# Expert weights of the last stage issued from SyncE behind each tile's value copies instead of from GpSimd

## The chip, the cores and the metric

One Trainium2 chip, one core of it. The time is the device time of one launch of the whole kernel in microseconds (us), the median of the runs shown.

## What is computed

Two transformer-like layers over x (64 batches of 32 tokens, 256 wide, so 2048 tokens), each with a cross attention, an attention and a feed-forward part. The change lies in the last two steps of the second layer: a causal grouped attention with 16 heads of 16 over 4 key/value groups, and a top-1 mixture of 8 experts.

```python
# attention of layer 1, on layernorm(x); g groups of keys and values, repeated for 4 heads each
kg = einsum('bse,ged->bgsd', x, Wk) + bk ; vg = einsum('bse,ged->bgsd', x, Wv) + bv
out = softmax(mask(q @ k.T / sqrt(16))) @ v
x = x + out
# experts of layer 1, on layernorm(x)
route = sigmoid(x @ router_w); e = argmax(route)
h = silu(x @ gate_w[e]) * (x @ up_w[e])          # 8 experts, 256 x 512 each
x = x + (h @ down_w[e]) * route[e]               # 512 x 256
```

The gate, up and down weights of one expert are 512 KB each in float32, so 4 MB for all gates, 4 MB for all ups and 4 MB for all downs.

## The kernel before, in words

The tokens lie in SBUF (`x_sb`) as 16 tiles of 128 rows, four batches of 32 tokens in a tile. Every stage of the kernel is one block in which each engine has its own instruction stream, and semaphores tie the streams together. The stage here is `attention_and_experts` (tensor names begin with `attn_` in the profile; `moe_gate`, `moe_up` and `moe_down` are the expert weights, `all_` and `w_` are tensors shared by stages). It runs from about 895 us to the end of the span.

**The attention half** is a software pipeline over the 16 tiles. In step i the TensorE stream does, in this order: scores of tile i (L2147, L2153), queries of tile i+1 (L2127), the transposes of the exponentials of tile i-1 (L2160), keys and values of tile i+1 (L2135, L2137), the transpose of the normalised tile i+2 (L2120), and last `weigh` of tile i-1 (L2171), the product of exponentials and values. The text calls the start of `weigh` of tile t W(t). The order is written out by hand in `step` of each engine; there is no scheduler.

**Values** take a detour. VectorE writes a tile's values (128 rows of 68 numbers, `v_rows`, L2407), SyncE copies them to DRAM (`v_stage`, L2001, 34 KB), waits until they have landed, and then issues four copies back into SBUF (`v_blocks`, L2005, 34 KB each), one for each of the four heads of a group, in the layout that `weigh` reads. `weigh` of tile t waits for these four copies. There are two buffers of each, so SyncE may start the four copies of tile t only when `weigh` of tile t-2 is done.

```python
for t in range(TILES):                       # SyncE before
    u = t % 2
    sp.wait_ge(s["v_ready"], t + 1)
    ...
    sp.dma_start(v_stage[u], ...)            # L2001
    sp.wait_ge(s["v_staged"], 16 * t + 16)
    wait_count(sp, s["o_made"], t - 1)
    for r in range(PER): sp.dma_start(v_blocks[u][...], v_stage[u]...)   # L2005, four
```

**Expert weights.** The gates are issued by SyncE at the end of the stage before (L2709, at 872 to 877 us). Ups and downs come from a generator, `load_ups_and_downs`, that issues one 512 KB load at each `next` (first the 8 ups, then the 8 downs, L2714). In the kernel before, GpSimd calls it twice in each of the iterations 1 to 8 of its own loop, right after it has normalised tile t (L2032). TensorE waits for all of them (`got_f`) only before the first expert slot, at about 1020 us.

**GpSimd** further adds the outputs of tile t-4 to x (L2037), writes the routing tables at iteration 3 (L2057 to L2063; VectorE waits for them in its step 0, L2457), and at the end computes the layernorm factors and the normalised rows (L140 to L147, L2042, L2077, L2079), after which ScalarE makes the rows of the middle tiles (L2328) and TensorE turns them (L2179) and routes (L2185).

**The expert half** begins at 1020 us: 23 slots, each with gate, up and down products (L2259, L2273).

Of the kernel before, what the change touches and what calls it, by code (L numbers as in the profile page):

```python
# [16 lines left out]
TILES = TOKENS // P  # L17
# [199 lines left out]
def wait_count(engine, semaphore, count):  # L217

    if not isinstance(count, int) or count > 0:
        engine.wait_ge(semaphore, count)  # L220
# [1674 lines left out]
EXPERTS, INNER = 8, 512  # L1895
# [3 lines left out]


def attention_and_experts(nc, name, scope, moments, x_sb, consts, ident, ident16, causal16, loaded, w, router_w, spare, room,
                          gate_w, up_w, down_w, load_pool, got_gates, got_f, out):


    sb, pb, sem = scope(name)
# [74 lines left out]
    def spare_of(n):  # L1980
        tiles = range(n * per_spare, min((n + 1) * per_spare, TILES))
        return tiles, spare[n][:, 0:len(tiles) * ROW].rearrange("p (t n) -> p t n", n=ROW)
# [9 lines left out]
    with nc.Block() as block:  # L1992

        @block.sync
        def _(sp):
            sp.wait_ge(s["blank"], 4)
            for t in range(TILES):
                u = t % 2
                sp.wait_ge(s["v_ready"], t + 1)
                wait_count(sp, s[f"v_in{u}"], 64 * (t // 2))  # L2000
                sp.dma_start(v_stage[u], v_rows[u][:, :, :].rearrange("p g d -> p (g d)")).then_inc(s["v_staged"], 16)  # L2001
                sp.wait_ge(s["v_staged"], 16 * t + 16)
                wait_count(sp, s["o_made"], t - 1)
                for r in range(PER):
                    sp.dma_start(v_blocks[u][SEQ * r:SEQ * r + SEQ, :, r, :, :].rearrange("k b g d -> k b (g d)"),  # L2005
                                 v_stage[u].rearrange("(b k) n -> k b n", b=TB)).then_inc(s[f"v_in{u}"], 16)

            out_tiles = out.rearrange("(t p) n -> p t n", p=P)
            for first, last in ((0, 12), (12, TILES)):
                sp.wait_ge(s["x_ready"], last)  # L2010
                sp.dma_start(out_tiles[:, first:last, :], x_sb[:, first:last, :]).then_inc(s["out_stored"], 16)

            normed_tiles = normed.rearrange("(t p) n -> p t n", p=P)
            for n in range(3):
                tiles, buffer = spare_of(n)
                wait_rows(sp, tiles[-1])
                if n == 1:
                    wait_rows(sp, EARLY[-1])
                if n == 2:
                    wait_rows(sp, MIDDLE[-1])  # L2020
                sp.wait_ge(s["prob_ready"], n + 2)
                sp.dma_start(normed_tiles[:, tiles.start:tiles.stop, :], buffer).then_inc(s["normed_stored"], 16)

        @block.gpsimd
        def _(pool):
            g = nc.gpsimd

            def normalise(t):
                if t == TILES - 1:
                    pool.wait_ge(s["dve_roots"], Moments.LAST_LINKS)  # L2030
                wait_count(pool, s["turned"], t)
                g.tensor_scalar(xn[:, :], x_sb[:, t, :], moments.moments[:, t, 0:1], moments.factors[:, t:t + 1],  # L2032
                                ALU.subtract, ALU.mult).then_inc(s["xn_ready"], 1)

            def add_outputs(t):
                pool.wait_ge(s["o_ready"], t + 1)
                g.tensor_tensor(x_sb[:, t, :], x_sb[:, t, :], outs[:, :, :].rearrange("p h d -> p (h d)"), ALU.add)\  # L2037
                 .then_inc(s["x_ready"], 1)

            def early_row(t):  # L2040
                pool.wait_ge(s["early_roots"], Moments.POOL_LINKS)
                g.tensor_scalar(rows(t), x_sb[:, t, :], moments.moments[:, t, 0:1], moments.factors[:, t:t + 1],  # L2042
                                ALU.subtract, ALU.mult).then_inc(s["early_rows"], 1)

            normalise(0)
            for u in range(2):
                g.memset(v_blocks[u][:, :, :, :, :], 0.0).then_inc(s["blank"], 1)
                g.memset(v_rows[u][:, :, HD], 1.0).then_inc(s["blank"], 1)
            loads = load_pool(pool)
            for t in range(1, TILES + POOL_LEAD - 1):  # L2050
                if t < TILES:
                    normalise(t)
                if t <= EXPERTS:
                    next(loads)
                    next(loads)
                if t == 3:
                    g.iota(count_rows[:, :], [[1, P]], 0, 0).then_inc(s["counted"], 1)  # L2057
                    g.iota(count_tiles[:, :], [[1, TILES]], -TILES, 0).then_inc(s["counted"], 1)
                    g.iota(count_p[:, :], [[1, 1]], 0, 1).then_inc(s["counted"], 1)
                    g.memset(ones16[:, :], 1.0).then_inc(s["tables16"], 1)  # L2060
                    g.memset(own16[:, TILES, :], 0.0).then_inc(s["tables16"], 1)
                    for u in range(2):
                        g.memset(x_in[u][:, :], 0.0).then_inc(s["x_in_clear"], 1)  # L2063
                if t >= POOL_LEAD:
                    add_outputs(t - POOL_LEAD)
                if t - POOL_LEAD == 10:
                    pool.wait_ge(s["early_stats"], 1)
                    pool.wait_ge(s["xn_ready"], len(EARLY))
                    moments.pool_roots(pool, s["early_roots"], EPS_LN, 1.0, EARLY)
                if t - POOL_LEAD in (11, 12, 13):  # L2070
                    for e in range(3 * (t - POOL_LEAD - 11), min(3 * (t - POOL_LEAD - 10), len(EARLY))):
                        early_row(e)
            pool.wait_ge(s["middle_stats"], 1)
            pool.wait_ge(s["xn_ready"], TILES)
            moments.pool_roots(pool, s["middle_roots"], EPS_LN, 1.0, MIDDLE)
            m = slice(MIDDLE.start, MIDDLE.stop)
            g.tensor_tensor(negated_mean[:, m], moments.moments[:, m, 0], moments.factors[:, m], ALU.mult).then_inc(s["mean_ready"], 1)  # L2077
            pool.wait_ge(s["mean_ready"], 1)
            g.tensor_scalar(negated_mean[:, m], negated_mean[:, m], -1.0, None, ALU.mult).then_inc(s["mean_ready"], 1)  # L2079

            def gather(j):
                g.indirect_dma_start(x_in[j % 2][:, :], None, normed, bass.IndirectOffsetOnAxis(token[:, j:j + 1], 0),
                                     bounds_check=TOKENS - 1, oob_is_err=False).then_inc(s[f"x_got{j % 2}"], 16)

            pool.wait_ge(s["x_in_clear"], 2)
            pool.wait_ge(s["normed_stored"], 16 * 3)
            pool.wait_ge(s["token_ready"], 1)
            gather(0)
            gather(1)
            pool.wait_ge(s["out_stored"], 32)  # L2090
            for j in range(SLOTS + 2):
                if j + 2 < SLOTS:
                    pool.wait_ge(s["x_turned"], j + 1)
                    pool.wait_ge(s["prob_kept"], j + 1)
                    gather(j + 2)
                if j >= 2:
                    pool.wait_ge(s["y_ready"], j - 1)
                    g.indirect_dma_start(out, bass.IndirectOffsetOnAxis(token[:, j - 2:j - 1], 0), y_out[j % 2][:, :], None,
                                         bounds_check=TOKENS - 1, oob_is_err=False, compute_op=ALU.add)\
                     .then_inc(s[f"y_stored{j % 2}"], 16)  # L2100
            for u in range(2):
                pool.wait_ge(s[f"y_stored{u}"], 16 * ((SLOTS + 1 - u) // 2))
# [450 lines left out]
def program(nc, d, out):  # L2553
# [9 lines left out]
    with outer:  # L2563
# [44 lines left out]
        got_gates, got_f = sem("got_gates"), sem("got_f")  # L2608

        era1 = outer.enter_context(ExitStack())  # L2610
        sb1, _, _ = scope("w", era1)
# [11 lines left out]
        def chunks(ap):  # L2623
            return ap.rearrange("(c p) n -> p c n", p=P)
# [36 lines left out]
        sb2, _, _ = scope("raw", era2)  # L2661
# [42 lines left out]
        sb3, _, _ = scope("moe", era3)  # L2704
# [3 lines left out]
            for e in range(EXPERTS):  # L2708
                sp.dma_start(f_gate[:, e, :, :], chunks(d["f_gate"][e])).then_inc(got_gates, 16)  # L2709

        def load_ups_and_downs(pool):
            for dst, src in ((f_up, d["f_up"]), (f_down, d["f_down"])):
                for e in range(EXPERTS):
                    pool.dma_start(dst[:, e, :, :], chunks(src[e])).then_inc(got_f, 16)  # L2714
                    yield

        phase = ExitStack()
# [95 lines left out]
```

## Time and profile before

| | |
|---|---|
| time, median of 3 runs | 1171.3 us (1168.67, 1171.3, 1177.4) |
| span of the profiled execution, first to last instruction | 1170.2 us |
| TensorE busy | 1105.2 us (94%) |
| attention half of the last stage | about 895 to 1004 us |
| expert half | about 1020 us to the end |

The profile shows one execution. Its span leaves out what lies around it; the median is 1.1 us above the span. A row of an engine's timeline gives the start, the time from the first start to the last end of the instructions on it, engine, line, operation, operands, how many, and in brackets how long the engine stood idle before and who released it.

### The profile page before, as it was taken

To read this page: it belongs to the slowest core of one execution; us is meant where nothing else is said; L and a number is where in the kernel's file an instruction comes from. 1 tells how busy PE (TensorE), PEld (TensorE's weight loads), DVE (VectorE), ACT (ScalarE), POOL (GpSimd) and SP (SyncE) were. 2 spreads that over 40 slices of the span, in tenths; PEclk is the share of its full clock that TensorE was granted. 3 is DMA by queue.
4 is the path that set the end of the run, shared out by engine and by line. 5 is a ranking of instruction groups with operands and counts; after the bars stand their busy time and mean duration, and the time that the engine had idled before them with its cause. 6 is when DMAs were issued, how large, how long until landed. Compare 5 with 4: busy or idle time off the path is not lost. (4 is left out here: it accounts for less than half of the span.)

```text
span 1170.2 us, 32565 instructions
## 1 busy us (share of the span) xinstructions
PE 1105.2 (94%) x12592; PEld 853.7 (73%) x12593; DVE 700.9 (60%) x1802; ACT 469.2 (40%) x1359; POOL 309.1 (26%) x421
## 2 busy tenths in 40 slices
PE   7998999999999899999979999999998798899996
PEld 6776878887887679889766777777765687556664
DVE  6897635445464665555448788887785587322221
ACT  2453535344352311212155565565552466222221
POOL 1701000000000000000253654655623547034442
PEclk9899999999999999999989999999999899799998
DMA  8631000000000055000101121121224643212211
GB/s 254 182 87 33 1 1 0 0 0 0 0 0 1 1 119 156 0 0 1 38 10 51 36 56 45 37 54 28 56 73 159 200 108 100 83 28 34 36 27 11
DMA packets 60205, 61.57 MB, mean 53 GB/s; under 512 B 26862, under 2 KB 51087, under 8 KB 59628
## 3 DMA queue, kind: packets, MB, share of 16 engines
q1 hardware_dynamic: 51836, 41.35, 13.3%
q0 software_dynamic: 8304, 19.32, 6.3%
q8 instruction: 45, 0.74, 0.3%
q14 instruction: 20, 0.16, 0.1%
HBM read 52.33 MB, written 10.14 MB: 53 GB/s over the span
## 5 line engine op out<-in xcount | busy, mean ns | idle before, releaser
L1729 ACT ACTIVATE xattn_exps<-xattn_ps_s,xattn_top 128x256 f32<-128x256 f32 x256 | 118.0, 475 | 76.9 <-DVE xattn_top L1797 76.9
L765 PEld LDWEIGHTS attn_ps_q<-attn_xnT,w_b_q 128*128 128x128 f32 x1024 | 118.8, 193 | 12.6 <-issue 12.6
L765 PE MATMUL attn_ps_q<-attn_xnT,w_b_q 128*128 128x128 f32 x1024 | 123.4, 276 | 0.0
L1255 POOL TENSOR_TENSOR fold_last_cos<-raw_last,all_consts 64x64 f32<-64x64 f32 x1 | 0.3, 317 | 453.5 <-POOLq L1063 453.5
L819 PE MATMUL attn_ps_out<-w_b_o,attn_oT 128*128 128x256 f32 x480 | 106.5, 380 | 1.8 <-DVE all_x L1000 1.5
L819 PEld LDWEIGHTS attn_ps_out<-w_b_o,attn_oT 128*128 128x128 f32 x480 | 90.0, 190 | 15.1 <-DVE all_x L1000 2.3
L873 ACT COPY attn_qT<-attn_ps_q 128x512 f32<-128x512 f32 x64 | 38.0, 594 | 148.2 <-PE attn_ps_q L765 148.2
L1804 DVE STREAM_TRANSPOSE xattn_expsT<-xattn_exps 128x1024 f32<-128x1024 f32 x64 | 79.5, 1241 | 22.9 <-ACT xattn_exps L1729 22.9
L1794 DVE TENSOR_REDUCE xattn_raw_top<-xattn_ps_s 128x4 f32<-128x1024 f32 x64 | 77.8, 1216 | 15.7 <-PE xattn_ps_s L1621 15.5
L1621 PE MATMUL xattn_ps_s<-xattn_kT,xattn_qT 64*32 64x256 f32 x2048 | 69.6, 381 | 2.9 <-ACT xattn_exps L1729 2.9
L1631 PE MATMUL xattn_ps_o<-xattn_expsT,xattn_kv 32*64 32x256 f32 x2048 | 64.1, 380 | 4.9 <-DVE xattn_last_scores L1840 3.5
L951 DVE BATCH_NORM_STATS2 attn_out_stats<-attn_ps_out 128x6 f32<-128x256 f32 x15 | 6.5, 432 | 99.6 <-PE attn_ps_out L819 99.6
L1596 PEld LDWEIGHTS xattn_ps_o<-xattn_xnT,all_d_a 128*128 128x128 f32 x512 | 61.5, 197 | 6.2 <-issue 6.2
L1596 PE MATMUL xattn_ps_o<-xattn_xnT,all_d_a 128*128 128x128 f32 x512 | 65.5, 283 | 0.0
L1631 PEld LDWEIGHTS xattn_ps_o<-xattn_expsT,xattn_kv 32*64 32x64 f32 x2048 | 44.4, 131 | 24.2 <-issue 11.9
L1094 PE MATMUL ffn_ps_h<-ffn_xnT,all_c 128*128 128x128 f32 x512 | 61.1, 278 | 0.0
L1111 PE MATMUL ffn_ps_out<-all_c,ffn_masked 128*128 128x256 f32 x256 | 59.6, 379 | 0.0
L1659 PE MATMUL xattn_ps_o<-all_d_b,xattn_ctxT 128*128 128x256 f32 x240 | 55.1, 382 | 4.4 <-POOL xattn_ctxT L1547 3.0
L1094 PEld LDWEIGHTS ffn_ps_h<-ffn_xnT,all_c 128*128 128x128 f32 x512 | 58.5, 192 | 0.0
L2544 DVE COPY all_d_b<-attn_ps_pT 128x512 f32<-128x512 f32 x23 | 15.9, 692 | 67.0 <-PE attn_ps_pT L2266 48.6
L1547 POOL TENSOR_TENSOR xattn_ctxT<-xattn_weighed_sum,xattn_inverse 128x256 f32<-128x256 f32 x60 | 42.8, 745 | 46.9 <-DMA xattn_inverse<-xattn_inverse_rows 46.9
L1621 PEld LDWEIGHTS xattn_ps_s<-xattn_kT,xattn_qT 64*32 64x32 f32 x2048 | 33.7, 106 | 27.3 <-issue 12.7
(359 smaller groups left out, 2322.0 us busy)
## 6 DMA issues: line engine op xcount, KB each, us to landing
xattn_inverse<-xattn_inverse_rows SPq DMA_DIRECT2D x30, 256.0 KB, 3.9
all_c<-in_ctx SPq DMA_DIRECT2D x64, 64.0 KB, 1.8
moe_gate<-in_f_gate SPq DMA_DIRECT2D x8, 512.0 KB, 8.1
moe_up<-in_f_up POOLq DMA_DIRECT2D x8, 512.0 KB, 5.2
moe_down<-in_f_down POOLq DMA_DIRECT2D x8, 512.0 KB, 5.5
xattn_v_stage<-xattn_v_rows SPq DMA_DIRECT2D x16, 136.0 KB, 2.0
xattn_v_blocks<-xattn_v_stage SPq DMA_DIRECT2D x64, 34.0 KB, 1.9
attn_v_blocks<-attn_v_stage SPq DMA_DIRECT2D x64, 34.0 KB, 1.9
```

Source lines behind the costliest of these rows:

```text
L765: last = nc.tensor.matmul(ps_q[g % 2][:, h * P:(h + 1) * P], wq[:, c, head * DH:(head + 1) * DH], xnT[u][:, c, :], start=(c == 0), stop=(c ...
L819: last = nc.tensor.matmul(bank[:, 0:DIM], of_heads[:, h, :, :].rearrange("p b q -> p (b q)"), wo[:, h, :], start=(h == 0), stop=(h == HEAD ...
L1094: last = nc.tensor.matmul(ps_h[half][:, j * P:(j + 1) * P], w1[:, c, f * P:(f + 1) * P], xnT[:, c, :], start=(c == 0), stop=(c == KC - 1))
L1111: last = nc.tensor.matmul(ps_out[:, 0:DIM], masked[u][:, f, :], w2[:, f, :], start=(f == 0), stop=(f == chunks - 1))
L1547: last = nc.gpsimd.tensor_tensor(ctxT[:, :, b, :], weighed_sum[:, :, b, :], inverse[:, b, :].rearrange("p (m q) -> p m q", q=SEQ), ALU.mult)
L1596: last = nc.tensor.matmul(ps_q[part][:, n * P:(n + 1) * P], a_w[:, c, m * P:(m + 1) * P], xnT[:, c, :], start=(c == 0), stop=(c == KC - 1))
L1621: last = nc.tensor.matmul(ps_s[g % 2][SEQ * b:SEQ * b + SEQ, 512 * odd + nkeys * n:512 * odd + nkeys * (n + 1)], qT[u][rows, b, 2 * g + n, :],
L1631: nc.tensor.matmul(ps_o[b][64 * odd:64 * odd + 64, 0:DIM], kv[u][rows, j, :], expsT[u][rows, :, odd, :, j, :], start=(j == 0), stop=False, ...
L1659: last = nc.tensor.matmul(out_bank(t), ctxT[:, m, :, :].rearrange("p b s -> p (b s)"), b_w[:, m, :], start=(m == 0), stop=(m == pairs - 1))
L1729: nc.scalar.activation(exps[g % 2][:, nkeys * k:nkeys * (k + 1)], ps_s[g % 2][:, nkeys * k:nkeys * (k + 1)], ACT.Exp, bias=top[u][:, n:n + ...
L1794: nc.vector.tensor_reduce(of_group(raw_top), ps_s[g % 2][:, :].rearrange("p (o m n) -> p o m n", o=2, m=2), X_AXIS, ALU.max, negate=True). ...
L1804: nc.vector.transpose(expsT[u][:, g, :, :, :, :].rearrange("p o m j q -> p (o m j q)"), exps[g % 2][:, :])\
```

## The change

The 16 loads of ups and downs leave GpSimd's loop. SyncE makes the generator's calls now: after the four value copies of tile t it issues no load for tiles 0 and 1, one for tiles 2 to 13, two for tiles 14 and 15. The order ups first, then downs, stays.

```diff
 def attention_and_experts(..., load_pool -> load_experts, ...)
         @block.sync
         def _(sp):
+            loads = load_experts(sp)
+
+            def loads_behind(t):
+                return 0 if t < 2 else 1 if t < TILES - 2 else 2
+
             sp.wait_ge(s["blank"], 4)
             for t in range(TILES):
...
                 for r in range(PER):
                     sp.dma_start(v_blocks[u][SEQ * r:SEQ * r + SEQ, :, r, :, :].rearrange("k b g d -> k b (g d)"),
                                  v_stage[u].rearrange("(b k) n -> k b n", b=TB)).then_inc(s[f"v_in{u}"], 16)
+                for _ in range(loads_behind(t)):
+                    next(loads)
...
-            loads = load_pool(pool)
             for t in range(1, TILES + POOL_LEAD - 1):
                 if t < TILES:
                     normalise(t)
-                if t <= EXPERTS:
-                    next(loads)
-                    next(loads)
...
-        def load_ups_and_downs(pool):
+        def load_ups_and_downs(sp):
             for dst, src in ((f_up, d["f_up"]), (f_down, d["f_down"])):
                 for e in range(EXPERTS):
-                    pool.dma_start(dst[:, e, :, :], chunks(src[e])).then_inc(got_f, 16)
+                    sp.dma_start(dst[:, e, :, :], chunks(src[e])).then_inc(got_f, 16)
                     yield
```

On SyncE, the first tiles of the stage before: the store of a tile's values and its four copies back follow each other with nothing between.

```order
L2001 DMA attn_v_stage<-attn_v_rows 128x68
L2005 DMA attn_v_blocks<-attn_v_stage 32x4x68 x4
L2001 DMA attn_v_stage<-attn_v_rows 128x68
L2005 DMA attn_v_blocks<-attn_v_stage 32x4x68 x4
L2001 DMA attn_v_stage<-attn_v_rows 128x68
```

On SyncE after the change, the last four tiles of the stage and what follows them (tiles 12 to 15; lines are 5 further down, `moe_` is the load).

```order
L2010 DMA attn_v_blocks<-attn_v_stage 32x4x68 x4
L2717 DMA moe_down<-in_f_down 128x4x256
L2006 DMA attn_v_stage<-attn_v_rows 128x68
L2010 DMA attn_v_blocks<-attn_v_stage 32x4x68 x4
L2717 DMA moe_down<-in_f_down 128x4x256
L2006 DMA attn_v_stage<-attn_v_rows 128x68
L2010 DMA attn_v_blocks<-attn_v_stage 32x4x68 x4
L2717 DMA moe_down<-in_f_down 128x4x256 x2
L2006 DMA attn_v_stage<-attn_v_rows 128x68
L2010 DMA attn_v_blocks<-attn_v_stage 32x4x68 x4
L2717 DMA moe_down<-in_f_down 128x4x256 x2
L2018 DMA out<-all_x 128x12x256
```

A load now stands between the value copies of one tile and the value store of the next, from tile 2 on; two stand there ahead of tile 15 and ahead of the stores of the output.

On GpSimd before, iterations 1 to 4 of its loop: a pair of loads follows each normalised tile, and the tables of iteration 3 stand behind the third pair.

```order
L2032 TENSOR_SCALAR attn_xn<-all_x,all_moments,all_moments_work 128x256
L2714 DMA moe_up<-in_f_up 128x2x512 x2
L2032 TENSOR_SCALAR attn_xn<-all_x,all_moments,all_moments_work 128x256
L2714 DMA moe_up<-in_f_up 128x2x512 x2
L2057 IOTA attn_count_rows 128x128
L2058 IOTA attn_count_tiles 128x16
L2059 IOTA attn_count_p 128x1
```

On GpSimd after, the same place.

```order
L2039 TENSOR_SCALAR attn_xn<-all_x,all_moments,all_moments_work 128x256 x3
L2060 IOTA attn_count_rows 128x128
L2061 IOTA attn_count_tiles 128x16
L2062 IOTA attn_count_p 128x1
```

The tables now follow the third normalised tile directly; the 16 load instructions are gone from this engine.

## Rows read from the trace of the kernel before

**Rows 1.** Busy time by stretch: us, engines' busy us (instructions), clock share, DMA, GB/s
```profile
912.00:924.00 12.00, 8.95 (x152) 7.41 (x152) 9.33 (x23) 7.18 (x20) 6.61 (x9) 1.00 0.72 221
924.00:936.00 12.00, 8.90 (x162) 7.21 (x163) 5.17 (x13) 3.58 (x11) 4.62 (x7) 0.72 0.50 132
...
948.00:960.00 12.00, 11.93 (x254) 9.62 (x254) 9.42 (x27) 8.25 (x23) 5.43 (x6) 1.00 0.23 44
...
927.00:932.00 5.00, 4.92 (x77) 3.95 (x78) 2.48 (x6) 0.16 (x1) 0.72 (x1) 0.52 0.68 203
```

**Rows 2.** TensorE's timeline: weigh of tiles 0 to 3, 7, 8, 14, and one query wait
```profile
911.30 0.68 PE L2171 MATMUL attn_ps_o<-attn_v_blocks,attn_expsT 128*32 128x68 f32 x32 [0.52 <-DMA attn_v_blocks<-attn_v_stage]
...
914.25 0.71 PE L2127 MATMUL attn_ps_q<-attn_xnT,all_e_q 128*128 128x128 f32 x4 [1.35 <-ACT attn_xnT L2299]
...
918.27 0.68 PE L2171 MATMUL attn_ps_o<-attn_v_blocks,attn_expsT 128*32 128x68 f32 x32 [0.76 <-DMA attn_v_blocks<-attn_v_stage]
...
927.08 1.14 PE L2171 MATMUL attn_ps_o<-attn_v_blocks,attn_expsT 128*32 128x68 f32 x32 [4.02 <-DMA attn_v_blocks<-attn_v_stage]
...
933.92 0.68 PE L2171 MATMUL attn_ps_o<-attn_v_blocks,attn_expsT 128*32 128x68 f32 x32
...
953.35 0.68 PE L2171 MATMUL attn_ps_o<-attn_v_blocks,attn_expsT 128*32 128x68 f32 x32
...
958.16 0.68 PE L2171 MATMUL attn_ps_o<-attn_v_blocks,attn_expsT 128*32 128x68 f32 x32
...
985.75 0.68 PE L2171 MATMUL attn_ps_o<-attn_v_blocks,attn_expsT 128*32 128x68 f32 x32 [0.30 <-issue]
```

**Rows 3.** SyncE's timeline: value stores and copies of tiles 2, 6 and 9
```profile
913.44 0.34 SPq L2001 DMA_DIRECT2D attn_v_stage<-attn_v_rows  x1
919.69 3.28 SPq L2005 DMA_DIRECT2D attn_v_blocks<-attn_v_stage  x4
...
938.72 0.34 SPq L2001 DMA_DIRECT2D attn_v_stage<-attn_v_rows  x1
942.39 1.73 SPq L2005 DMA_DIRECT2D attn_v_blocks<-attn_v_stage  x4
...
953.33 0.34 SPq L2001 DMA_DIRECT2D attn_v_stage<-attn_v_rows  x1
954.85 1.73 SPq L2005 DMA_DIRECT2D attn_v_blocks<-attn_v_stage  x4
```

**Rows 4.** The page's DMA issues: KB each, median us from issue to landing
```profile
xattn_inverse<-xattn_inverse_rows SPq DMA_DIRECT2D x30, 256.0 KB, 3.9
...
attn_v_blocks<-attn_v_stage SPq DMA_DIRECT2D x64, 34.0 KB, 1.9
```

**Rows 5.** Two downs on GpSimd at 935 us, and the gates: us from issue to landing
```profile
L2714 POOL DMA_DIRECT2D moe_down<-in_f_down x2: 760/784/809, 935.2 to 936.0; - x2
DMA to landing us min/median/max: 4.6/5.3/5.9
...
L2709 SPq DMA_DIRECT2D moe_gate<-in_f_gate x8: 469/540/792, 872.3 to 876.9; - x8
...
DMA to landing us min/median/max: 5.4/8.1/10.8
```

**Rows 6.** Stretches as in Rows 1: a pair of 256 KB loads; seven gates
```profile
855.00:857.60 2.60, 2.60 (x50) 2.13 (x30) 2.56 (x8) 1.54 (x6) 1.35 (x2) 1.00 0.78 212
...
877.70:886.00 8.30, 7.58 (x100) 5.38 (x99) 4.40 (x9) 2.05 (x9) 0.73 (x2) 1.00 1.03 380
```

**Rows 7.** GpSimd's and VectorE's timelines at the tables; GpSimd's and TensorE's at the end
```profile
907.90 1.49 POOL L2714 DMA_DIRECT2D moe_up<-in_f_up  x2
...
909.88 0.74 DVE L2457 CAST attn_of_row<-attn_count_rows 128x128 f32<-128x128 int32 x1 [3.48 <-POOL attn_count_p L2059]
...
988.37 0.73 POOL L2037 TENSOR_TENSOR all_x<-all_x,attn_outs 128x256 f32<-128x256 f32 x1 [0.30 <-DVE attn_outs L2416]
...
994.44 0.69 PE L2179 MATMUL attn_ps_kv<-all_consts,all_c 128*128 128x128 f32 x2 [2.02 <-ACT all_c L2328]
```

More of the change, by code:

```diff
@@ L1901, in attention_and_experts @@
 def attention_and_experts(nc, name, scope, moments, x_sb, consts, ident, ident16, causal16, loaded, w, router_w, spare, room,
-                          gate_w, up_w, down_w, load_pool, got_gates, got_f, out):
+                          gate_w, up_w, down_w, load_experts, got_gates, got_f, out):
     sb, pb, sem = scope(name)
```

## The prediction

> **What bounds the kernel now.** TensorE is busy 94% of the span, so I looked only for places where it is not, or where it is slow, in the stretch that the change touches. The view by stretches comes first [rows 1]: from 948 to 960 us TensorE is busy 11.93 of 12 us, while between 912 and 936 it is busy 8.95 and 8.90 of 12, and of the second 12 us it had only 0.72 of its clock. The DMA share is 0.72 and 0.50 there against 0.23 later: the 16 loads of ups and downs run in the poor stretch and not in the good one. Next TensorE's timeline [rows 2]. The start of `weigh`, W(t), is the pulse of the pipeline. W(8) minus W(7) is 958.16 - 953.35 = 4.81 us; the next gap in the steady part is 4.9, so I take 4.85 as the step when nothing is late. The first steps are W(1)-W(0) = 6.97, W(2)-W(1) = 8.81 and W(3)-W(2) = 6.84 us. The brackets name the causes: 0.52, 0.76 and 4.02 us of waiting for the value copies, and 1.35 us for ScalarE's xnT. After the 4.02 us of idleness the granted clock is 0.52 from 927 to 932, that is, the lower of its two levels (1.2 instead of 2.4 GHz) for most of it, and `weigh` takes 1.14 instead of 0.68 us.
>
> SyncE's timeline says why the copies are late [rows 3]. With no load in flight the store of tile 9 is issued at 953.33 and its copies at 954.85: 1.5 us for the store to land. For tile 6 it is 3.7 us (938.72 to 942.39), for tile 2 it is 6.2 us (913.44 to 919.69), and the four copies then take 3.28 us to issue instead of 1.73. The loads were issued by GpSimd and not by SyncE; yet the store of tile 6 lands at 942.4, just behind the second of two downs (936.0 + 5.9 = 941.9) [rows 5]. So a value store in effect waits until the loads ahead of it are in.
>
> **Part 1, GpSimd loses its loads.** The tables of iteration 3 stood behind a pair of loads of 1.49 us [rows 7], and VectorE stood idle 3.48 us until the tables were there, before it could turn the scores of tile 1. The tables come 1.49 us earlier, and VectorE's shift, ScalarE's exponentials and xnT behind it with them: of TensorE's 1.35 us about 0.9 goes (TensorE itself arrives 0.52 earlier at that point, so about 0.45 of waiting remains). Other pairs on GpSimd (7 of them, 1.5 us each) lay beside waits of GpSimd for TensorE and cost nothing.
>
> **Part 2, no loads beside the values of tiles 0 to 2.** Stores 0, 1 and 2 are free of ups and downs. The waits of 0.52, 0.76 and 4.02 us go, and with the idle gap the slow clock: W(3)-W(2) falls from 6.84 to 4.81, another 2.03. What is late next there is nothing, since a store that lands in 1.5 us puts a tile's copies in SBUF a full step before `weigh` wants them. Sum of the gain: 0.52 + 0.9 + 0.76 + 4.02 + 2.03 = 8.2 us. W(14), at 985.75 before, would be at 977.55.
>
> **Part 3, what the loads cost where they go.** They now stand in SyncE's own chain: four copies of tile t (1.73 us of issue, plus 0.04), the load, the store of tile t+1, and SyncE waits until that store has landed before it issues the copies of t+1. Call L the time from the issue of the load to the landing of the store behind it. One turn of SyncE takes 1.77 + L. TensorE's step is 4.85, so SyncE keeps up if L is at most 3.1; above that it falls behind by L - 3.1 a tile and uses up the slack first.
>
> The start: values of tile 2 are ready at about 912.0 (1.45 earlier than 913.4), the store lands 1.5 later at 913.5, and the load of tile 2 is issued at 915.3. The copies of tile 3 begin at 915.3 + L, those of tile 14 eleven turns later, and their last copy lands 3.3 later (it is issued 1.3 after the first and takes 1.9 [rows 4]). So W(14) is the later of 977.55 and 915.3 + L + 11 (1.77 + L) + 3.3 = 938.1 + 12 L. Fully hidden up to L = 3.29; even with before at L = 3.97; each 0.1 us of L is 1.2 us of time in between. I count to tile 14, since its output sets GpSimd's last addition at 988.37, the factors behind it and TensorE's restart at 994.44 [rows 7]; tile 15, which stands behind two loads, has the 2.02 us for which TensorE waits there as cover, and its extra (one more load, 1.4 us, and the longer turn, 0.8) just fits into that.
>
> L does not occur in the trace, since nothing was queued behind a single 512 KB load on SyncE. From below: a store alone takes 1.5, and the gates, eight in a row on SyncE's queue, land 1.43 us apart (872.3 + 5.4 = 877.7 to 876.9 + 10.8 = 887.7, over seven) [rows 5], so L is at least 1.5 + 1.4 = 2.9. From above: the first of a pair on GpSimd landed after 4.6 us, and store 6 landed 0.5 behind its load, so 5.1. The nearest row is a pair of 256 KB loads on SyncE (3.9 us to land [rows 4], the second issued 0.6 after the first, so 4.5 us for 512 KB). Their bytes moved in 2.6 us at 212 GB/s, the gates at 380 [rows 6], at which 524 thousand bytes take 1.4 us: 1.2 less, so a load lands after 3.3 and the store behind it 0.5 later, as store 6 did. This row is nearer than the ends, having the same queue and the same bytes, and I take L = 3.8: W(14) = 983.7, 2.1 us earlier than before. The issue itself, 0.5 to 0.6 us [rows 5], lies within L.
>
> For the landing of one load the Trainium skill ("DMA: Bandwidth & Descriptors", Anatomy of one DMA) fits 2.0 us plus the bytes over 436 GB/s, measured for GpSimd's path; as an estimate that is 3.2 us for 512 KB. The quicker of the two downs on GpSimd took longer, 4.6 [rows 5]. By the page L would be 3.7 and the gain 3.3 us in place of 2.1.
>
> **Part 4, the rest.** The output stores stand behind two loads (about 3 us); they are needed only by the expert half's additions after 1020 us. The last load is issued at about 990 and lands before 1000; TensorE wants it at 1020. Both cost nothing.
>
> **The rivals.**
> A, the forecast: SyncE's chain eats most of the gain, L from 3.4 to 4.2, that is 6.9 us earlier to 2.7 later, 1164.4 to 1174; 50%.
> B, the load is hidden: L up to 3.4. The lower bound 2.9 speaks for it, and that only one load is in flight at a time. Gain 6.9 to 8.2, 1163.1 to 1164.4. A bonus is possible: if TensorE's clock falls in the 2.02 us wait before 994.44 [rows 7], as it did after the 4.02 us, and tile 15 now fills that wait, the clock may hold. The slow level cost 2.0 us in a step of 6.84, so 3 us in the ten up to 1004, and the products behind it a little more. 22%, of which 4 with that and a time below 1159.6.
> C, slower: the SyncE chain becomes the bound of every step. The mechanism is the closed loop copies, load, store, landing; the price 12 us for each us of L; it decides from L = 3.97 on. For it speaks that stores took 3.7 to 6.2 us whenever loads were near. L from 4.2 to 5.1 gives 2.7 to 13.6 later, 1174 to 1185; 18%, 3 of them past 1%.
> D, the same loop with TensorE idle about 1 us in every step lets the clock fall, as the 4.02 us did; at the lower level a step costs 2.0 us more (6.84 against 4.81), over ten steps 20: about 1190. Against it: 1.35 us idle at 912.9 did not lower it (clock share 1.00 to 924). 7%.
> E, the loads were not what held the stores. The Trainium skill (same page, Queues, rings and completion order) says that each DMA engine takes turns between queues packet by packet, so that loads in GpSimd's queue should hardly delay a store in SyncE's, while in SyncE's own the store is behind the whole load; that speaks against this change. The row shows otherwise: 3.7 us against 1.5 with loads in the other queue, landing just behind them. If it held nevertheless, worked out from rows, the stall at 923 stays, L is the lower bound and hidden, and only the 0.9 of part 1 is won: 1170.4. 3%.
>
> **How the numbers follow.** The likeliest case is A at L = 3.8: 2.1 us off. The sum is made on the profiled span of 1170.2; carried over to the median of 1171.3 it gives 1169.2 us. The range takes B without its bonus and C up to L = 4.6: 1161 to 1179; outside it lie the bonus, D and the top of C, some 16%. One per cent, 11.7 us, is about what a measurement of this kernel can tell from no change. Faster by more: 4%. Slower by more (D and the top of C): 10%. Within: 86%.
>
> **What would show it.** In the changed profile no wait for `attn_v_blocks` at tiles 0 to 2 and a clock share of 1.00 from 900 to 936; the wait of VectorE for the tables 1.5 shorter. From tile 3 on the distance from a load's issue to the next copies on SyncE is L; if it is above 3.3, TensorE's waits for the value copies start after some tiles and repeat in each step, with W(t) going at 1.77 + L. If the copies are in time everywhere, B holds. The prediction is wrong if L is over 4.6, if the clock drops in the new short waits, or if the loads, moved later, touch something that I have called free.

## Result, and the profile after

| | before | after |
|---|---|---|
| time, median of 17 runs each | 1173.41 us | 1181.28 us |
| ratio to before, 95% interval | 1 | 1.0071, 1.0055 to 1.0086 |
| span of the profiled execution | 1170.2 us | 1177.1 us |

The change costs 0.7%, some 8 us. I had forecast a gain of 2 us (1169.2 us, range 1161 to 1179), with a loss of 3 to 14 us as rival C at 18% and one of about 20 us as rival D at 7%. The measured 1181.28 us lies above the range and within rival C.

TensorE's timeline after the change, the starts of `weigh` (compare [rows 2]):

```profile
912.73 0.68 PE L2174 MATMUL attn_ps_o<-attn_v_blocks,attn_expsT 128*32 128x68 f32 x32
...
914.85 0.71 PE L2130 MATMUL attn_ps_q<-attn_xnT,all_e_q 128*128 128x128 f32 x4 [0.51 <-ACT attn_xnT L2302]
...
918.12 0.68 PE L2174 MATMUL attn_ps_o<-attn_v_blocks,attn_expsT 128*32 128x68 f32 x32
922.93 0.68 PE L2174 MATMUL attn_ps_o<-attn_v_blocks,attn_expsT 128*32 128x68 f32 x32
...
938.00 0.68 PE L2174 MATMUL attn_ps_o<-attn_v_blocks,attn_expsT 128*32 128x68 f32 x32 [0.36 <-DMA attn_v_blocks<-attn_v_stage]
943.98 0.68 PE L2174 MATMUL attn_ps_o<-attn_v_blocks,attn_expsT 128*32 128x68 f32 x32 [1.19 <-DMA attn_v_blocks<-attn_v_stage]
949.69 0.68 PE L2174 MATMUL attn_ps_o<-attn_v_blocks,attn_expsT 128*32 128x68 f32 x32 [0.81 <-DMA attn_v_blocks<-attn_v_stage]
...
987.46 0.68 PE L2174 MATMUL attn_ps_o<-attn_v_blocks,attn_expsT 128*32 128x68 f32 x32 [3.67 <-DMA attn_v_blocks<-attn_v_stage]
...
992.22 1.14 PE L2174 MATMUL attn_ps_o<-attn_v_blocks,attn_expsT 128*32 128x68 f32 x32 [0.31 <-DMA attn_v_blocks<-attn_v_stage]
...
1001.46 1.13 PE L2174 MATMUL attn_ps_o<-attn_v_blocks,attn_expsT 128*32 128x68 f32 x32 [2.45 <-DMA attn_v_blocks<-attn_v_stage]
...
1005.35 0.69 PE L2182 MATMUL attn_ps_kv<-all_consts,all_c 128*128 128x128 f32 x2 [0.31 <-ACT all_c L2331]
```

The early stall is gone: tiles 0 to 2 wait for nothing (4.02 us before), and the wait for xnT (the turned normalised tile that ScalarE writes) is 0.51 instead of 1.35. VectorE's wait for the tables fell from 3.48 to 1.95 us, the 1.5 that part 1 of the prediction had put:

```profile
910.25 0.73 DVE L2460 CAST attn_of_row<-attn_count_rows 128x128 f32<-128x128 int32 x1 [1.95 <-POOL attn_count_p L2062]
```

In place of the early stall stand waits for the value copies from tile 5 on, about 1 us in every tile, 3.67 us at tile 13 and 2.45 at tile 15. SyncE's timeline shows where they come from (compare [rows 3]):

```profile
914.03 0.34 SPq L2006 DMA_DIRECT2D attn_v_stage<-attn_v_rows  x1
916.35 1.73 SPq L2010 DMA_DIRECT2D attn_v_blocks<-attn_v_stage  x4
918.12 0.43 SPq L2717 DMA_DIRECT2D moe_up<-in_f_up  x1
918.65 0.41 SPq L2006 DMA_DIRECT2D attn_v_stage<-attn_v_rows  x1
922.94 1.74 SPq L2010 DMA_DIRECT2D attn_v_blocks<-attn_v_stage  x4
...
942.49 0.43 SPq L2717 DMA_DIRECT2D moe_up<-in_f_up  x1
943.02 0.41 SPq L2006 DMA_DIRECT2D attn_v_stage<-attn_v_rows  x1
946.39 1.74 SPq L2010 DMA_DIRECT2D attn_v_blocks<-attn_v_stage  x4
...
976.08 1.74 SPq L2010 DMA_DIRECT2D attn_v_blocks<-attn_v_stage  x4
...
982.76 1.74 SPq L2010 DMA_DIRECT2D attn_v_blocks<-attn_v_stage  x4
...
988.97 1.74 SPq L2010 DMA_DIRECT2D attn_v_blocks<-attn_v_stage  x4
990.74 0.98 SPq L2717 DMA_DIRECT2D moe_down<-in_f_down  x2
991.83 0.46 SPq L2006 DMA_DIRECT2D attn_v_stage<-attn_v_rows  x1
996.79 1.75 SPq L2010 DMA_DIRECT2D attn_v_blocks<-attn_v_stage  x4
```

From 918.65 on SyncE never waits for VectorE: each store is issued right behind the load, and then SyncE waits for it. From the first load at 918.12 to the copies of tile 14 at 988.97 there are 12 loads and 11 sets of copies: (70.85 - 11 x 1.78) / 12 = 4.27 us in the mean for L (3.9 to 4.9 in single turns), where I had taken 3.8. A turn takes 1.78 + 4.27 = 6.05 us, TensorE's step 4.85. The landing times of the ups on SyncE (tile view; us from issue to landing, least, middle, most) say that nearly all of L is the load itself:

```profile
L2717 SPq DMA_DIRECT2D moe_up<-in_f_up x8: 433/434/436, 918.1 to 960.0; - x8
...
DMA to landing us min/median/max: 3.7/3.9/4.3
```

The four downs issued at tiles 10 to 13 took a little longer, 4.0 to 4.7 us (median 4.2).

The view by stretches (columns as in [rows 1]) shows the clock:

```profile
899.50:904.00 4.50, 4.41 (x23) 4.13 (x23) 0.97 (x2) 1.84 (x7) 0.76 (x2) 0.62 0.00 0
938.00:984.00 46.00, 38.30 (x734) 31.79 (x734) 31.87 (x84) 25.76 (x72) 23.61 (x34) 1.00 0.44 119
984.00:987.46 3.46, 0.00 (x0) 0.00 (x0) 0.39 (x2) 1.13 (x4) 1.25 (x2) 1.00 0.59 145
987.46:996.00 8.54, 8.23 (x124) 7.26 (x125) 4.80 (x16) 2.60 (x6) 5.18 (x8) 0.57 0.58 165
...
1034.00:1042.00 8.00, 8.00 (x26) 4.05 (x27) 1.45 (x4) 2.85 (x5) 1.99 (x2) 1.00 0.07 18
```

The short waits did not lower it (1.00 from 938 to 984, with TensorE busy 38.3 of 46 us). Behind the long one at tile 13 it fell: 0.57.

To compare executions whose earlier stages differ by some us, the text below counts from the first transpose of this stage (896.84 us before, 897.22 after) and ends at the first expert product (1023.99 and 1033.88). I call that the half: 127.2 us before, 136.7 after, 9.5 more. The stages ahead add 0.4, and the expert half is 3.0 shorter (146.2 to 143.2), which together give the 6.9 of the spans. Before, the expert half began at a clock share of 0.79, after the change at 1.00:

```profile
1024.00:1032.00 8.00, 8.00 (x21) 3.92 (x22) 0.97 (x3) 2.58 (x4) 1.71 (x2) 0.79 0.01 2
```

I can't put this down to the change: the same 8 us are at 0.79 in the variant below that differs from the changed kernel only in the place of one load behind tile 14.

### The profile page after: what moved, and what is told of

It is laid out like the page before. It is cut to its first block and busy times, and to the rows that moved or that the text cites. A ratio compares the mean times of both kernels' runs of the same rounds, so it can differ in the third digit from the quotient of the medians.

```text
span 1177.1 us, 32565 instructions
## 1 busy us (share of the span) xinstructions
PE 1107.2 (94%) x12592; PEld 858.8 (73%) x12593; DVE 701.4 (60%) x1802; ACT 468.7 (40%) x1359; POOL 296.9 (25%) x405
## 5 line engine op out<-in xcount | busy, mean ns | idle before, releaser
L1804 DVE STREAM_TRANSPOSE xattn_expsT<-xattn_exps 128x1024 f32<-128x1024 f32 x64 | 79.5, 1242 | 22.4 <-ACT xattn_exps L1729 22.4
```

Of the source, the lines that this page charges most:

```text
L1804: nc.vector.transpose(expsT[u][:, g, :, :, :, :].rearrange("p o m j q -> p (o m j q)"), exps[g % 2][:, :])\
```

## Experiments

All are variants of the changed kernel. The profile figures are of one execution each; the ratios rest on 7 to 10 executions of a variant (17 of the changed kernel, one of the last variant), against 17 to 28 of the kernel before that were run beside them. Two theories stand against each other. **Closed loop:** the loss is SyncE's own chain, a store behind a load on the queue on which SyncE waits. **Contention:** loads slow the value transfers wherever they are queued.

| run | half, us | weigh of tile 0, from the start of the half | weigh of tile 14, from the start of the half | ratio to before (95%) |
|---|---|---|---|---|
| before | 127.2 | 14.5 | 88.9 | 1 |
| after | 136.7 | 15.5 | 95.0 | 1.0071 (1.0055 to 1.0086) |
| store first, then load | 120.2 | 14.0 | 81.0 | 0.9934 (0.9904 to 0.9963) |
| half a load per tile | 121.2 | 14.0 | 81.3 | 0.9940 (0.9908 to 0.9972) |
| all loads behind tile 15 | 128.7 | 15.3 | 82.3 | 0.9977 (0.9953 to 1.0001) |
| GpSimd, one per tile | 125.2 | 16.3 | 85.7 | 0.9966 (0.9934 to 0.9999) |
| one load at tile 14 | 136.5 | 15.2 | 96.1 | 1.0057 (1.0033 to 1.0080) |
| store first, none near tiles 14, 15 | 119.6 | 15.3 | 82.3 | 0.9929 (0.9900 to 0.9958) |
| a load from tile 0 on | 139.4 | 15.5 | 99.3 | one run, 1188.94 us |

The column for tile 0 is there because the executions differ already before the changed kernel's first load (in the kernel before, 0.5 of the 14.5 us is waiting for the copies): from the start of the half to this `weigh` the clock share was 1.00 in the kernel before and in the two variants at 14.0 us, 0.89 or 0.79 in all others. So up to 2.3 us of a difference at tile 14 can come from the clock at the start, and the safer count is from tile 0: 74.5 us to tile 14 before, 79.5 after, 67.0 with the store first, 67.0 with all loads last.

### Store first, then the load

```diff
                 sp.dma_start(v_stage[u], ...)
+                if t > 0:
+                    for _ in range(loads_behind(t - 1)): next(loads)
                 sp.wait_ge(s["v_staged"], 16 * t + 16)
...
-                for _ in range(loads_behind(t)):
-                    next(loads)
```

> The changed kernel with one thing turned round: SyncE issues the store of tile t+1 first and the load of tile t right behind it, so the load is in flight while SyncE waits for the store, and the copies of t+1 come behind the load. Closed-loop theory (the loss is SyncE's own turn: copies, load, then a store that lands only after the load): the store lands in 1.5 to 2.0 us again, a turn of SyncE is about 4 us and below TensorE's 4.85, no wait for the value copies repeats, weigh of tile 14 comes at 978 to 981 us instead of 992.2, and the time is 6 to 12 us below the changed kernel, ratio to before 0.992 to 0.999. Contention theory (a load beside the value transfers slows them wherever it stands): stores still take 3.5 us or more, TensorE waits 0.8 to 1.2 us in each tile as now, ratio 1.004 to 1.010.

Measured: 1165.57 us, ratio 0.9934. The ratio is 0.0137 below that of the changed kernel, some 16 us, more than the 6 to 12 that I had put. The half is 16.5 us shorter than after, of which 1.5 had come before the first `weigh`. SyncE's timeline of this kernel:

```profile
946.78 0.34 SPq L2006 DMA_DIRECT2D attn_v_stage<-attn_v_rows  x1
947.16 0.43 SPq L2721 DMA_DIRECT2D moe_up<-in_f_up  x1
948.69 1.74 SPq L2013 DMA_DIRECT2D attn_v_blocks<-attn_v_stage  x4
951.59 0.34 SPq L2006 DMA_DIRECT2D attn_v_stage<-attn_v_rows  x1
```

The same load at the same tile in the same queue, and the store is in after 1.9 us; SyncE is free at 950.4 and waits 1.2 us for the next values. TensorE's `weigh` keeps its pace to tile 14:

```profile
946.79 0.68 PE L2178 MATMUL attn_ps_o<-attn_v_blocks,attn_expsT 128*32 128x68 f32 x32
951.60 0.68 PE L2178 MATMUL attn_ps_o<-attn_v_blocks,attn_expsT 128*32 128x68 f32 x32
...
984.96 1.13 PE L2178 MATMUL attn_ps_o<-attn_v_blocks,attn_expsT 128*32 128x68 f32 x32 [1.17 <-DMA attn_v_blocks<-attn_v_stage]
```

The closed loop is shown, and contention as the cause of the loss falls: only the order of two issues differs. The load does still slow what stands behind it, since the copies now land 2.0 to 3.6 us after their issue (median 2.8, from 925 to 975 us) instead of 1.7 to 2.0 after the change, but they are needed only some 8 us after they begin. Only tile 15, whose copies stand behind a pair of loads, still waits, 1.17 us.

### Half a load per tile

```diff
-                return 0 if t < 2 else 1 if t < TILES - 2 else 2
+                return 0 if t < 2 else 1 if t < TILES - 2 else 2 if t < TILES - 1 else 18
...
-                    sp.dma_start(dst[:, e, :, :], chunks(src[e])).then_inc(got_f, 16)
-                    yield
+                    for c in range(2):       # half of the chunks each, h = number of chunks / 2
+                        sp.dma_start(dst[:, e, c * h:(c + 1) * h, :], chunks(src[e])[:, c * h:(c + 1) * h, :]).then_inc(got_f, 16)
+                        yield
```

> The changed kernel with half a load (256 KB) in the place of each load behind tiles 2 to 14, and the other 16 halves plus two behind tile 15. It measures how much of L, the time from the issue of a load to the landing of the store behind it (4.27 us in the mean in the changed kernel), goes by bytes. If it is transfer time at the gates' 380 GB/s, L falls by 0.7 to about 3.6 and weigh of tile 14 comes 8 us earlier than in the changed kernel, near 984. If L is a fixed price of a DMA standing in front (descriptors, landing), it stays above 4.1 and weigh of tile 14 stays at 990 or later. Total, ratio to before: 0.995 to 1.001 in the first case, 1.004 to 1.010 in the second.

SyncE's timeline of this kernel:

```profile
928.30 0.43 SPq L2719 DMA_DIRECT2D moe_up<-in_f_up  x1
928.84 0.38 SPq L2006 DMA_DIRECT2D attn_v_stage<-attn_v_rows  x1
931.37 1.74 SPq L2010 DMA_DIRECT2D attn_v_blocks<-attn_v_stage  x4
```

L is 3.07 us here and 3.15 in the mean of the twelve tiles 3 to 14, so 256 KB less take off 1.12 us, not the 0.7 that the gates' rate gives: a rate of 234 GB/s. `weigh` of tile 14 comes 13.7 us earlier than after (1.5 of it before tile 0), not 8, since a turn of 4.93 us almost keeps TensorE's step: the slack lasts until tile 14, which waits 0.69 us, and tile 15, which waits 1.69. The ratio, 0.9940, is just below the range that I had given. Within these sizes L goes by bytes, and more steeply than I had it. With the two-load turn after (990.74 to 996.79, 6.05 us) the three sizes are 3.15, 4.27 and 6.05 us for 256, 512 and 1024 KB.

### All loads behind tile 15

```diff
-                return 0 if t < 2 else 1 if t < TILES - 2 else 2
+                return 16 if t == TILES - 1 else 0
```

> The changed kernel with all 16 loads behind the value copies of tile 15, ahead of the output stores: no load beside any value transfer. It shows the step of TensorE without loads from tile 0 on, and so what the full gain of part 1 and 2 of the prediction is. Both theories: no wait for value copies at all, weigh of tile 14 at 977 to 980. The 8 MB then need about 22 us from 985 on, the output stores and the stores of the normalised rows stand behind them until about 1019, so 2 to 6 us of the gain may be given back before the first gather. Ratio to before 0.993 to 1.000. If the clock at the pipeline's start or something else and not the loads made the early stall, weigh of tile 14 would stay at 984 or later.

No `weigh` waits for its copies, and tile 14 comes 82.3 us into the half against 88.9 before; on that count the early stall was the loads' doing. But the half ends later than before, for the stores of the normalised rows, which the first gather reads, stand behind 8 MB (TensorE's timeline):

```profile
1022.67 0.66 PE L2257 MATMUL attn_ps_T<-all_consts,attn_x_in 128*128 128x128 f32 x2 [10.73 <-DMA attn_x_in<-normed,attn_token]
```

I had put 2 to 6 us for what is given back; it is 8.5 against the kernel with the store first (128.7 - 120.2), of which 1.3 are there before tile 0. The interval of the ratio (0.9953 to 1.0001) does not tell this kernel from the one before.

### GpSimd, one load per tile

```diff
-            loads = load_experts(sp)          # and loads_behind, and its calls on SyncE
...
+            loads = load_experts(pool)
             for t in range(1, TILES + POOL_LEAD - 1):
                 if t < TILES:
                     normalise(t)
+                for _ in range(0 if t < 4 or t > 17 else 1 if t < 16 else 2):
+                    next(loads)
```

> One load per tile, from tile 4 on, as in the changed kernel, but issued by GpSimd behind its normalise: the rate of the change without its queue and without SyncE's chain. Closed-loop theory: a load in GpSimd's queue is not followed by SyncE's store in the same chain, so delays of a store (0 to 1.5 us) do not add up; at most single waits for value copies, weigh of tile 14 at 978 to 982. GpSimd is the engine that sets the end of the attention half, so its 6 loads in the last iterations, 0.78 us each, come on top there, up to 4.7 us. Ratio 0.995 to 1.001. Contention theory: waits for the copies of 0.8 to 1.2 us in each tile from tile 6 on as in the changed kernel, ratio 1.004 or more.

The rate of the change, in the other queue: no wait for copies to tile 13. Stores do land later while loads are near (1.8 to 2.7 us from 925 to 970 us, against 1.5 to 1.6 without loads), but the delays don't add up, since SyncE is not held beyond the one store. What it costs came at the end, and larger than I had put it. Beside the pair of loads issued at 977.7 and 978.5 us the last copy of tile 14 lands 5.6 us after its issue and the store of tile 15 takes 6.6 us (3.0 in the kernel before, with no load near), and TensorE waits 2.68 us at tile 14 and 1.21 at tile 15. SyncE's and TensorE's timelines:

```profile
978.93 0.39 SPq L2001 DMA_DIRECT2D attn_v_stage<-attn_v_rows  x1
985.49 1.73 SPq L2005 DMA_DIRECT2D attn_v_blocks<-attn_v_stage  x4
```

```profile
983.99 0.68 PE L2170 MATMUL attn_ps_o<-attn_v_blocks,attn_expsT 128*32 128x68 f32 x32 [2.68 <-DMA attn_v_blocks<-attn_v_stage]
990.99 1.14 PE L2170 MATMUL attn_ps_o<-attn_v_blocks,attn_expsT 128*32 128x68 f32 x32 [1.21 <-DMA attn_v_blocks<-attn_v_stage]
```

So there is contention, from loads in another queue, when two stand together, as before the change. One per tile, from either queue, made no `weigh` wait in these kernels where SyncE did not wait behind it.

### One load at tile 14 instead of two

```diff
-                return 0 if t < 2 else 1 if t < TILES - 2 else 2
+                return 0 if t < 2 else 1 if t < TILES - 1 else 3
```

> The changed kernel with one load instead of two behind tile 14, and three instead of two behind tile 15. It sizes the term of tile 15, which the prediction had put under cover. If the second load in front of tile 15 is on the path (it lengthened SyncE's last turn to 6.05 us of L against 4.3), weigh of tile 15 comes 1.8 us earlier counted from weigh of tile 14 and the time falls by 1.5 to 2.5 us against the changed kernel, more where the products after it run at the lower clock. If it was covered, weigh of tile 15 moves but the first expert product does not. Ratio to before 1.003 to 1.007.

`weigh` of tile 15 comes 7.1 us behind tile 14 instead of 9.2, and TensorE restarts 3.89 us behind it in both kernels:

```profile
1001.28 1.14 PE L2174 MATMUL attn_ps_o<-attn_v_blocks,attn_expsT 128*32 128x68 f32 x32 [0.27 <-DMA attn_v_blocks<-attn_v_stage]
1005.17 0.69 PE L2182 MATMUL attn_ps_kv<-all_consts,all_c 128*128 128x128 f32 x2 [0.31 <-ACT all_c L2331]
```

So tile 15 is on the path and has no cover left. Of the 2.2 us little is seen in the half (0.2), because tile 14 itself came 1.1 later in this execution and from TensorE's restart to the first expert product it took 1.0 more (29.5 against 28.5), with more of it at the lower clock. The two ratios, 1.0057 and 1.0071, have intervals that overlap: the size is not settled by them.

### Store first, no load near tiles 14 and 15

```diff
-                return 0 if t < 2 else 1 if t < TILES - 2 else 2
+                return 0 if t < 1 or t > 12 else 2 if t in (4, 6, 8, 10) else 1
```

(made in the kernel with the store first)

> Store first, then the load, as in the experiment with the store ahead, but with all 16 loads behind the stores of tiles 2 to 13 (one each, two at four of them), none near tiles 14 and 15. That experiment still had 1.17 us of waiting at tile 15, behind two pairs of loads. Closed-loop theory: two loads behind one store lengthen the landing of one tile's copies by 1.8 us, inside their slack of a step, so no wait for value copies anywhere, weigh of tile 15 4.5 us after tile 14, and the first expert product 0 to 3 us earlier than there, counted from the start of the stage; ratio to before 0.990 to 0.995. Contention theory: waits at the tiles with two loads, no gain over it.

The only wait for copies left is 0.37 us at tile 14, tile 15 follows after 4.5 us, and the half is 0.6 us shorter than with the store first alone. At 1165.59 us and 0.9929 the two cannot be told apart; either beats the kernel before.

```profile
986.19 0.68 PE L2178 MATMUL attn_ps_o<-attn_v_blocks,attn_expsT 128*32 128x68 f32 x32 [0.37 <-DMA attn_v_blocks<-attn_v_stage]
990.68 0.68 PE L2178 MATMUL attn_ps_o<-attn_v_blocks,attn_expsT 128*32 128x68 f32 x32
994.83 0.44 PE L2186 MATMUL attn_ps_kv<-all_consts,all_c 128*128 128x128 f32 x2 [2.02 <-ACT all_c L2335]
```

### A load from tile 0 on

```diff
-                return 0 if t < 2 else 1 if t < TILES - 2 else 2
+                return 1
```

> The changed kernel with one load behind each of the 16 tiles, also tiles 0 and 1 and never two. A test of the loop's arithmetic: a turn with a load takes 1.78 + 4.27 = 6.05 us wherever it stands. The copies of tile 2 then begin 2.2 us later than in the changed kernel (two turns from 905.6 on instead of TensorE's pace), weigh of tile 14 comes 2 us later, tile 15 follows one single-load turn, 6 us, behind it instead of 9, so that the first expert product is within 1.5 us of the changed kernel's, counted from the start of the stage. If a turn is bound by anything that TensorE's pace sets, weigh of tile 14 stays where it is and the end comes 2 us earlier.

The copies of tile 2 begin 22.2 us into the half (19.1 after, so 3.0 later, not 2.2), the twelve turns from there to tile 14 take 6.17 us each (999.01 - 924.99), and TensorE waits from tile 2 on. `weigh` of tile 14 is 4.3 us later than after, where I had expected 2, and the half 2.8 longer, where I had said within 1.5: the first turns were longer (6.9 us), with one issue of copies of 2.77 us and one of a load of 1.50, for which I have no cause. From the copies of tile 0 to those of tile 3 it takes 20.7 us against 17.4 after, from there to tile 14 67.2 against 66.0. That tile 14 comes later and not at the same time speaks for SyncE's turn as the bound; the size is not as I had worked it out. It is a single execution.

## Why the prediction was wrong

**The early stall and its gain: right.** Waits of 0.52, 0.76 and 4.02 us and the slow clock behind them are gone, and the xnT wait fell by 0.84 (0.9 forecast). With nothing in the way, the kernels with the store first and with all loads last bring tile 14 to 81.0 and 82.3 us into the half against 88.9, a gain of 6.6 to 7.9 where the sum said 8.2. Counted from tile 0 both gain 7.5, where the sum, without its 0.52 for tile 0, said 7.7.

**The closed loop: right in kind.** `weigh` of tile 14 is set by SyncE's turns, and putting the load on the other side of the store removes it. That is the mechanism of rival C as well; the forecast and C differ only in the size of L.

**L: the step that failed.** "a load lands after 3.3 and the store behind it 0.5 later ... I take L = 3.8". The loads landed after 3.9 (ups) to 4.2 us (downs, medians) and L was 4.27. I had scaled the transfer part to the rate of eight gates in a row (380 GB/s); a single load between small copies costs by its bytes as at 234 GB/s. Twelve times 0.47 is 5.6 us, and the break-even was 3.97.

**The start of the loop.** I had the first load 18.5 us after the first transpose; it came at 20.9, 2.4 later. Of this 1.6 is there before the store of tile 2 is issued (16.8 us in, where I had 15.2): the wait of 0.52 at tile 0 went, but `weigh` of tile 0 came 1.05 later than before all the same, with a clock share of 0.62 from 899.5 to 904. That part differs from execution to execution: the variants of the changed kernel had 14.0 to 16.3 us for it. The store of tile 2 took 2.3 us, though no load was near (1.5 expected), which is 0.8; the kernel with all loads last has it too, at 2.9. Forecast -2.1, plus 5.6, plus 2.4, gives +5.9; measured for tile 14 is 95.0 - 88.9 = +6.1.

**Tile 15: the second wrong step.** "its extra ... just fits into that" 2.02 us wait. `weigh` of tile 15 came 9.24 us behind tile 14, not 4.55: 4.7 us more, and not the 2.2 that I had put, which was itself more than the 2.02 of cover. Of the 9.24, 7.82 is SyncE's turn with two loads, and the rest is that the copies took 1.4 us longer to land. The cover is gone (TensorE now goes on 3.89 us behind tile 15 with 0.31 of waiting), so 10.8 us of delay at tile 15 leave 9.5 in the half. I had not seen that TensorE's steps are shorter at the end (W(14)-W(13) was 3.35 before) while SyncE's turn is not. The wait of 3.67 us at tile 13 is another matter: the turn before it took 6.68 us (976.08 to 982.76), and the last of its four copies landed 3.4 us after its issue where 1.9 is usual. No run shows why these copies, and those of tile 15, took so long.

**The sum.** Forecast -2.1 at tile 14, 5.6 for L and 2.4 for the start, 3.4 more for tile 15, -3.0 in the expert half and 0.4 in the stages ahead give 6.7; the spans differ by 6.9, the medians by 7.9. The chances that I gave for the outside of the range were 4, 7 and 3%, which is 14 and not "some 16%".

**The clock: rival D fell, for the steps.** About 1 us of idleness in each left it at 1.00. It fell behind the long wait of tile 13. But the length of one wait does not decide it: with the store first it fell at tile 15, behind a wait of 1.17 us (`weigh` 1.13 instead of 0.68). The bonus of rival B was not tested: after the change the 2.02 us wait was filled, but the clock had been low since tile 13 (0.50 from 996 to 1005.35), and in the kernel with no load near tiles 14 and 15 the wait stayed and the clock was 0.55 behind it, as before (0.50 from 994.44 to 1004). The 3.0 us that the expert half gave back, with its first 8 us at 1.00 instead of 0.79, I had not foreseen, and why its clock was higher there is not settled.

**Rival E** fell: loads in GpSimd's queue delay stores in SyncE's, by 0.3 to 1.2 us when they stand alone, and by more beside a pair. The Trainium skill ("DMA: Bandwidth & Descriptors", Queues, rings and completion order) has, beside the turn-taking that I had quoted, that a semaphore's increment lands only after every earlier write of that DMA engine across its queues. A store of 6.6 us beside GpSimd's pair agrees with it: it landed at 985.4, the second load of the pair at 985.3 (978.5 + 6.8). No run here separates this from plain sharing. Part 4 held: no expert product waits for a weight.

## What to carry to other kernels

When an engine issues a transfer and then waits for it, everything that it issued just before is inside that wait; put bulk loads behind the transfer that is waited for, not in front. Here this order alone is the difference between 0.7% slower and 0.7% faster. Before moving bulk loads into such a chain, add up one turn of it and compare it with the step of the bounding engine, at the last tiles apart, where steps are shorter; near break-even an error of 0.5 us in one landing counts once per tile.

## What the hardware showed beyond expectation

A 512 KB load on SyncE, alone between small copies, took 3.7 to 4.7 us to land (median 3.9 for ups, 4.2 for downs); a small store behind 256, 512 and 1024 KB of loads landed 3.15, 4.27 and 6.05 us after the first of them was issued. A 34 KB store with no load near took 1.5 us in most tiles, but 2.0 to 2.9 at tile 2 and 3.0 to 3.2 at tile 15, the latter before the change too, and no run says why; the first four copies of the stage took 2.5 to 2.9 us to issue in every kernel after the change, in place of 1.76. The clock share from the first transpose of the stage to `weigh` of tile 0 was 0.79 in one of these executions (16.3 us), 0.89 in five (15.2 to 15.5 us) and 1.00 in three (14.0 to 14.5 us), with nearly the same instructions.
